# Dispatch tables of two MoE layers from 16-bit one-hot factors, with the tile as the innermost dimension

## The reference

```python
# layer 1
probs = softmax(x @ router_w.T)
w, sel = top_k(probs, 2);  w = w / sum(w)
out = sum over e of combine[:, e, None] * ((silu(x @ g[e]) * (x @ u[e])) @ d[e])
# layer 3: sigmoid router, relu experts with biases, plus a shared feed-forward
scores, idx = top_k(sigmoid(flat @ router_w.T), 2);  w = scores / (sum(scores) + 1e-6)
routed = sum over e of comb[:, e, None] * (relu(flat @ ew1[e] + eb1[e]) @ ew2[e] + eb2[e])
# both: x = x + tanh(g_ffn[l]) * out
```

## Time and profile before

| | us |
|---|---|
| three runs | 1659.20, 1656.66, 1650.44 (median 1656.66) |
| profiled execution, its own time | 1657.25 |
| its span, first to last instruction | 1655.5 |
| busy in the span: PE, PEld | 1409.8 (85%), 1303.3 (79%) |
| DVE, ACT, POOL | 1240.4 (75%), 765.6 (46%), 336.8 (20%) |
| mean granted TensorE clock | 0.906 of full |

### The profile page before, as it was taken

One profiled execution on the slowest core, in us unless ns is written; L12 is line 12 of the kernel. 1 busy time (PEld: TensorE's weight loads), 2 busy tenths in 40 slices (PEclk: granted clock), 3 DMA queues, 4 the chain that ended last, 5 costly groups with the idle time before them and its releaser, 6 DMA issues.

```text
span 1655.5 us, 26047 instructions
## 1 busy us (share of the span) xinstructions
PE 1409.8 (85%) x9986; PEld 1303.3 (79%) x9986; DVE 1240.4 (75%) x2386; ACT 765.6 (46%) x1306; POOL 336.8 (20%) x278
## 2 busy tenths in 40 slices
PE   4897998798996499999489558977999999999995
PEld 4786887586896389999379458966888888999995
DVE  5696778677795679998379779976885857888883
ACT  4445441013454167666355442316454225767673
POOL 2241001000000147765200000000000002445342
PEclk9897997799997589998799879988997999999997
DMA  4232100000002178887400000000002006777883
GB/s 138 89 103 91 41 1 1 1 0 10 1 1 108 52 249 233 241 227 214 127 1 1 7 1 1 1 3 8 1 1 103 1 32 256 218 227 209 227 240 114
DMA packets 44927, 148.24 MB, mean 90 GB/s; under 512 B 11651, under 2 KB 22582, under 8 KB 35062
## 3 DMA queue, kind: packets, MB, share of 16 engines
q1 hardware_dynamic: 28886, 122.04, 21.5%
q0 software_dynamic: 15936, 24.78, 7.7%
HBM read 126.03 MB, written 22.87 MB: 90 GB/s over the span
## 4 chain that ended last, share of the span: by engine, by line
PE 57%; DVE 25%; ACT 7%; issue 5%; DMA 3%; POOLq 1%; SPq 1%; POOL 0%; ACTq 0%; DVEq 0%
PE PS L307 36%; PE PS L1006 6%; PE PS L967 3%; PE PS L990 3%; DVE RA L1597 2%; PE PS L1072 2%; PE PS L1223 1%; DVE RA L1666 1%; DVE FA L1634 1%; ACT RA L1590 1%; PE PS L283 1%; PE PS L999 1%; DVE RA L1646 1%; PE PS L983 1%; ACT Y L225 1%
## 5 line engine op out<-in xcount | busy, mean ns | idle before, releaser
L307 PE MATMUL PS<-RA 128*128 128x256 f32 (+3 forms) x6204 | 945.7, 312 | 78.7 <-DVE RA L398 17.4
L307 PEld LDWEIGHTS PS<-RA 128*128 128x128 f32 x6204 | 862.0, 198 | 133.9 <-issue 34.2
L1524 POOL DMA_INDIRECT sum_rows<-Y,KT x78 | 158.2, 2028 | 191.1 <-ACT Y L1565 163.0
L271 POOL TENSOR_TENSOR rstd<-vareps,neghalf 128x4 f32<-128x4 f32 x36 | 36.8, 1023 | 712.2 <-DVE vareps L208 333.9
L1006 PE MATMUL PS<-VBF,FA 128*128 128x136 f32 x1024 | 137.4, 288 | 4.2 <-ACT FA L772 3.9
L1513 POOL DMA_INDIRECT Y<-normed_rows,KT x78 | 90.0, 1154 | 235.6 <-DVE KT L1316 170.7
L1006 PEld LDWEIGHTS PS<-VBF,FA 128*128 128x128 f32 x1024 | 126.1, 194 | 10.2 <-ACT FA L772 6.6
L772 ACT ACTIVATE FA<-PS 128x1024 f32<-128x1024 f32 x64 | 65.7, 1027 | 105.3 <-PE PS L967 105.3
L1597 DVE TENSOR_TENSOR RA<-FA,RA 128x2048 fp32r<-128x2048 f32 x46 | 105.3, 2288 | 8.5 <-ACT RA L1557 7.9
L1543 ACT ACTIVATE FA<-PS,unit_bias 128x256 f32<-128x256 f32 (+1 forms) x184 | 71.7, 445 | 78.4 <-PE PS L307 65.4
L1666 DVE TENSOR_TENSOR RA<-FA,RA 128x1024 fp32r<-128x1024 f32 (+1 forms) x46 | 80.9, 1759 | 24.8 <-ACT RA L1590 24.8
(11 more groups left out here) (292 smaller groups left out, 1917.4 us busy)
## 6 DMA issues: line engine op xcount, KB each, us to landing
FA<-in_eup SPq DMA_DIRECT2D x46, 1024.0 KB, 7.4
FA<-in_edown SPq DMA_DIRECT2D x23, 1024.0 KB, 6.6
FA<-in_edown SPq DMA_DIRECT2D x23, 512.0 KB, 4.1
FA<-in_fside SPq DMA_DIRECT2D x16, 512.0 KB, 3.5
sum_rows<-X SPq DMA_DIRECT2D x2, 2048.0 KB, 8.2
normed_rows<-Y SPq DMA_DIRECT2D x2, 2048.0 KB, 7.5
fp_rows<-FA POOLq DMA_DIRECT2D x6, 352.0 KB, 6.7
FA<-fp_rows SPq DMA_DIRECT2D x1, 2112.0 KB, 12.2
```

The costliest lines, as they stand in the source:

```text
L307: ins = pe.matmul(dst, stat(a, k), mov(b, k), start=(first and n == 0), stop=(last and n == len(todo) - 1))
L1524: pool.indirect_dma_start(out=sum_rows, in_=rows_out[p][:, t, :], in_offset=None, compute_op=ALU.add, out_offset=bass.IndirectOffsetOnAxis ...
```

## The change

The one-hot factors become 16-bit (bf16), and the tile becomes their innermost dimension: `lane_hot` is (k, lane, tile) and `col_hot` (part, column, tile). The two values of a column become five (`PARTS_OF_ROW`), each exact in 16 bits: the token as its partition number and its tile number plus 1, the weight as a high, a middle and a low part (`split_weights`, four operations that are new on VectorE's path, in layer 1 after `places_of_rows`, in layer 3 after `accumulate(0, 3)`). A set of factors is now three operations: a mask over 39 x 16 columns and tiles, one product of the mask with all five parts (5 x 39 x 16 = 3120 elements), and one lane comparison (128 x 16 = 2048). It signals `hot` once. TensorE runs one instruction per product, with 195 moving columns in place of 78; the elements of one tile are 16 elements (32 bytes) apart in both operands. `write_tables` puts the parts together again in nine operations. GpSimd's constants are written out over the tiles (2048, 624 and four of 16 elements).

```diff
+PARTS_OF_ROW = 5
...
@@ -1163,18 +1166,26 @@
...
-                self.lane = c[:, 0:P]
-                self.column = c[:, 128:128 + NROWS]
-                self.token = c[:, 176:176 + NT]
+                self.parts = c[:, 0:80].bitcast(BF16).rearrange("p (k v t) -> p k v t", k=2, v=PARTS_OF_ROW)
...
-                self.lane_hot = self.xn_all.rearrange("p t d -> p (t d)").rearrange("p (k t n) -> p k t n", k=2, n=P)
                 self.apart = router.kind == "top"
-                self.col_hot = [fview(3072 if self.apart else 7168, NT, 2, NROWS), fview(7168, NT, 2, NROWS)]
+                yf = self.xn_all.rearrange("p t d -> p (t d)")
+                self.lane_hot = yf[:, 0:NT * P].bitcast(BF16).rearrange("p (k n t) -> p k n t", k=2, n=P)
+                hots = PARTS_OF_ROW * NROWS * NT // 2
+                hot_of = lambda v: v.bitcast(BF16).rearrange("p (v c t) -> p v c t", v=PARTS_OF_ROW, c=NROWS)
+                first_hot = hot_of(yf[:, NT * P:NT * P + hots])
+                self.col_hot = [first_hot, hot_of(fview(7232, hots)) if self.apart else first_hot]
+                self.lane = fview(4096 if self.apart else 7168, NT * P // 2).bitcast(BF16).rearrange("p (n t) -> p n t", n=P)
...
+                self.mask = yf[:, NT * P + hots:NT * P + hots + NROWS * NT // 2].bitcast(BF16).rearrange("p (c t) -> p c t", c=NROWS)
...
@@ -1194,9 +1205,11 @@
...
-                pool.iota(self.lane, [[1, P]], base=0, channel_multiplier=0, allow_small_or_imprecise_dtypes=True)
-                pool.iota(self.column, [[1, NROWS]], base=0, channel_multiplier=0, allow_small_or_imprecise_dtypes=True)
-                pool.iota(self.token, [[1, NT]], base=1, channel_multiplier=NT, allow_small_or_imprecise_dtypes=True)
+                pool.iota(self.lane, [[1, P], [0, NT]], base=0, channel_multiplier=0, allow_small_or_imprecise_dtypes=True)
+                pool.iota(self.column, [[1, NROWS], [0, NT]], base=0, channel_multiplier=0, allow_small_or_imprecise_dtypes=True)
+                for k in range(2):
+                    pool.iota(self.parts[:, k, 0, :], [[0, NT]], base=0, channel_multiplier=1, allow_small_or_imprecise_dtypes=True)
+                    pool.iota(self.parts[:, k, 1, :], [[1, NT]], base=1, channel_multiplier=0, allow_small_or_imprecise_dtypes=True)
...
@@ -1217,10 +1230,10 @@
                 pe.matmul(self.counts(1), self.ones, both, start=True, stop=True).then_inc(self.counted, 1)
...
             def sum_tables(self, pe, k):
+                pe.wait_ge(self.hot, 2 * self.turn + k + 1)
                 for t in range(NT):
-                    if t % (NT // 2) == 0:
-                        pe.wait_ge(self.hot, 4 * self.turn + 2 * k + t // (NT // 2) + 1)
-                    ins = pe.matmul(PS[:, 7, 0:2 * NROWS], self.lane_hot[:, k, t, :], self.col_hot[k][:, t].rearrange("p v c -> p (v c)"),
+                    ins = pe.matmul(PS[:, 7, 0:PARTS_OF_ROW * NROWS].rearrange("p (v c) -> p v c", v=PARTS_OF_ROW),
+                                    self.lane_hot[:, k, :, t], self.col_hot[k][:, :, :, t],
                                     start=(k == 0 and t == 0), stop=(k == 1 and t == NT - 1))
                 ins.then_inc(self.summed, 1)
...
@@ -1287,33 +1300,42 @@
                     steps(dve.tensor_reduce(self.posf[:, k, :], self.pick, AX, ALU.add))
                 steps(dve.tensor_copy(rows_of[:, :, :], self.posf))
                 steps(dve.tensor_scalar(self.col_u.bitcast(U32), rows_of[:, :, :], 7, None, ALU.logical_shift_right))
-                steps(dve.tensor_copy(self.col_f, self.col_u.bitcast(U32)))
-                steps(dve.scalar_tensor_tensor(self.lane_f, self.col_f, -float(P), self.posf, ALU.mult, ALU.add))
+                steps(dve.tensor_copy(self.col_b, self.col_u.bitcast(U32)))
+                steps(dve.scalar_tensor_tensor(self.lane_b, self.col_b, -float(P), self.posf, ALU.mult, ALU.add))
...
             def one_hot(self, dve, steps, k):
                 dve.wait_ge(self.normed_out, 16 * (self.turn + 1))
                 if k and not self.apart:
                     dve.wait_ge(self.summed, 2 * self.turn + k)
-                wide = [P, NT, NROWS]
-                hot = self.col_hot[k]
-                steps(dve.tensor_tensor(hot[:, :, 0, :], self.column.unsqueeze(1).to_broadcast(wide),
-                                        self.col_f[:, k, :].unsqueeze(2).to_broadcast(wide), ALU.is_equal))
-                steps(dve.tensor_tensor(hot[:, :, 1, :], hot[:, :, 0, :], row_weight[:, k, :].unsqueeze(2).to_broadcast(wide), ALU.mult))
-                dve.tensor_tensor(hot[:, :, 0, :], hot[:, :, 0, :], self.token.unsqueeze(2).to_broadcast(wide), ALU.mult)
-                half = [P, NT // 2, P]
-                for q in range(2):
-                    ts = slice(q * NT // 2, (q + 1) * NT // 2)
-                    dve.tensor_tensor(self.lane_hot[:, k, ts, :], self.lane.unsqueeze(1).to_broadcast(half),
-                                      self.lane_f[:, k, ts].unsqueeze(2).to_broadcast(half), ALU.is_equal).then_inc(self.hot, 1)
+                if k:
+                    dve.wait_ge(self.hot, 2 * self.turn + k)
+                wide = [P, NROWS, NT]
+                of_columns = lambda v: v.unsqueeze(1).to_broadcast(wide)
+                steps(dve.tensor_tensor(self.mask, self.column, of_columns(self.col_b[:, k, :]), ALU.is_equal))
+                every = [P, PARTS_OF_ROW, NROWS, NT]
+                dve.tensor_tensor(self.col_hot[k], self.mask.unsqueeze(1).to_broadcast(every),
+                                  self.parts[:, k].unsqueeze(2).to_broadcast(every), ALU.mult)
+                dve.tensor_tensor(self.lane_hot[:, k], self.lane, self.lane_b[:, k, :].unsqueeze(1).to_broadcast([P, P, NT]),
+                                  ALU.is_equal).then_inc(self.hot, 1)
+
+            def split_weights(self, dve, steps):
+                steps(dve.tensor_copy(self.parts[:, :, 2, :], row_weight[:, :, :]))
+                steps(dve.tensor_tensor(self.left, row_weight[:, :, :], self.parts[:, :, 2, :], ALU.subtract))
+                steps(dve.tensor_copy(self.parts[:, :, 3, :], self.left))
+                steps(dve.tensor_tensor(self.parts[:, :, 4, :], self.left, self.parts[:, :, 3, :], ALU.subtract))
...
             def write_tables(self, dve, steps):
                 dve.wait_ge(self.summed, 2 * self.turn + 2)
-                ids, weights = PS[:, 7, 0:NROWS], PS[:, 7, NROWS:2 * NROWS]
-                dve.tensor_scalar(source_of, ids, -1.0, 0.0, ALU.add, ALU.max)
-                steps(dve.tensor_scalar(self.empty, ids, 0.0, None, ALU.is_equal))
+                lanes, tiles, high, middle, low = (PS[:, 7, v * NROWS:(v + 1) * NROWS] for v in range(PARTS_OF_ROW))
+                dve.tensor_copy(weight_of, low)
+                steps(dve.tensor_copy(self.ids, tiles))
+                dve.tensor_scalar(self.empty, self.ids, 0.0, None, ALU.is_equal)
+                dve.tensor_tensor(weight_of, weight_of, middle, ALU.add)
+                steps(dve.scalar_tensor_tensor(self.ids, lanes, float(NT), self.ids, ALU.mult, ALU.add))
+                dve.tensor_scalar(source_of, self.ids, -1.0, 0.0, ALU.add, ALU.max)
                 steps(dve.tensor_tensor(self.empty, self.empty, self.unused, ALU.mult))
-                dve.tensor_copy(weight_of, weights)
-                dve.scalar_tensor_tensor(target_of, ids, -1.0, self.empty, ALU.add, ALU.add).then_inc(self.tables, 1)
+                dve.tensor_tensor(weight_of, weight_of, high, ALU.add)
+                dve.scalar_tensor_tensor(target_of, self.ids, -1.0, self.empty, ALU.add, ALU.add).then_inc(self.tables, 1)
                 dve.wait_ge(self.tables, self.turn + 1)
...
         def route(l, kind):
@@ -1356,6 +1378,7 @@
                 router.weigh(dve, steps)
                 dispatch.blocks_of_experts(dve, steps)
                 dispatch.places_of_rows(dve, steps)
+                dispatch.split_weights(dve, steps)
                 for k in range(2):
                     dispatch.one_hot(dve, steps, k)
                 handover["first_up"](dve)
```

More of the change, by code:

```diff
@@ L1165, in __init__ @@
                 c = spare_const
-                self.lane = c[:, 0:P]
-                self.column = c[:, 128:128 + NROWS]
-                self.token = c[:, 176:176 + NT]
+                self.parts = c[:, 0:80].bitcast(BF16).rearrange("p (k v t) -> p k v t", k=2, v=PARTS_OF_ROW)
+                self.lane_b = c[:, 80:96].bitcast(BF16).rearrange("p (k t) -> p k t", k=2)
+                self.col_b = c[:, 96:112].bitcast(BF16).rearrange("p (k t) -> p k t", k=2)
+                self.left = c[:, 112:144].rearrange("p (k t) -> p k t", k=2)
+                self.ids = c[:, 144:144 + NROWS]
                 self.unused_pairs = c[:, 192:192 + NROWS + 1].rearrange("p (b h) -> p b h", h=BR // P)
@@ L1171, in __init__ @@
                 self.col_u = c[:, 240:272].rearrange("p (k t) -> p k t", k=2)
-                self.col_f = c[:, 272:304].rearrange("p (k t) -> p k t", k=2)
```

(8 more changed lines are left out.)

## The result

The changed kernel took 1662.66 us (median of 20 runs, 1657.21 to 1664.9) against 1655.27 for the kernel before (20 runs, 1649.82 to 1660.12): ratio 1.0043, 95% interval 1.0032 to 1.0055, or 7.1 us slower. The forecast was 1649.9 us. The profiled execution's span grew from 1655.5 to 1663.1 us.

The account below looks back on a forecast made before the run. Bound: first layer by VectorE's start plus TensorE's 32 products, second by TensorE's time per product. First layer -4.8 and second -2.0, together -6.8 on 1657.25, gave 1650.4; the runs' median, 0.6 lower, made it 1649.9 us (range 1643.5 to 1660).

Parts of the forecast that it names:

- TensorE: one instruction per product: Table sums, both MoE layers: one 195-column instruction replaces two, 159 ns a product at 2.4 GHz, 246 at 1.2.
- surcharge for the moving columns' step: TensorE's table products: 0.31 ns for each of 195 columns, 61 ns a product, taken from VectorE's stepped rows.
- The scaling by clock: TensorE's table products: unbroken columns scaled by 1.89 from 2.4 to 1.2 GHz, 98 to 185 ns a product.
- Rival B: Table products, both layers: TensorE pays VectorE's whole step rate, 326 ns at both clocks; sum +1.2 us, 1657.9; chance 0.17.
- VectorE's pace: Factor sets: 16-bit operations at 0.52 ns an element; mask 0.48, product 1.78, lanes 1.22 us, a set 3.44.
- The first layer's logic: First MoE layer: VectorE's first set, then TensorE's 32 products in 7.87 us, then tables; 4.8 us gained.
- The weight split: VectorE, four small operations: 0.88 us on the first layer's path, hidden in 1.36 us of idling in the second.
- The tables: Table writing: nine operations take 1.58 us, +0.70 on the first layer's path, inside 10.7 us of room in the second.
- Rival C: VectorE's factors: 16-bit operations run no faster, a set takes 6.45 us; sum +0.3 us, 1657.0; chance 0.06.
- Rival D: TensorE's products: the stepped weight load isn't hidden, 540 ns a product; sum +14.9 us, 1671.6; chance 0.06.
- Rival A: TensorE's products: the step costs nothing, 98 and 185 ns a product; sum -10.1 us, 1646.6; chance 0.26.
- Rival E: Behind the first layer's tables: its gain is swallowed downstream, say by weight loads; -2.0 us, 1654.7; chance 0.09.

Follow-up runs that it names:

- the doubled pairs: Changed kernel with tile outermost, each token's number stored twice, 40 unbroken columns a part: 1643.82 us, ratio 0.9944 to the kernel before.
- the plain kernel: Changed kernel with tile outermost, one copy of each token's number repeated by a step of zero, 195 unbroken columns: ratio 0.9974 to the kernel before.
- the two-tile kernel: Changed kernel with two tiles innermost instead of sixteen, so TensorE steps over 4 bytes, no number doubled: ratio 0.9951 to the kernel before.
- the 565.39 window: First-layer profile window of the changed kernel with six groups of 16 extra products ahead of the second half in both layers; whole time not compared.

## Why the prediction was wrong

**The step that failed is "TensorE: one instruction per product"**, in its surcharge for the moving columns' step: 0.31 ns a column was taken, for 159 ns a product at 2.4 GHz and 246 at 1.2. Measured: 359 and 364. A column costs 1.8 to 1.9 ns, which lies outside even the upper bound, VectorE's whole 1.67 (326 ns). The surcharge came from VectorE's rows; TensorE pays about four times its unbroken 85 ns. Its base was misread as well: the 14 elements of L1233 that stood for contiguous ones are seven pairs whose two values lie 32 bytes apart (line 1250 of the kernel before turns the two dimensions round), and they took 176 ns, so VectorE's own price of such a step was not settled by these rows. The scaling by clock was wrong too: a product with the 32-byte step takes about as long at either clock (359 ns mostly at 1.00, 364 at 0.50), while an unbroken one depends on it (16 in 1.39 us at 1.00 with the doubled pairs; in 2.81 at 0.50 in the plain kernel's first layer). The prediction's own sum turned to a loss from 308 ns a product; with the measured products it gives 11.66 + 5.75 + 5.76 - 19.7 = +3.5 us.

**Its consequence, the clock, was priced nowhere.** Of the 7.1 us in the second layer, 4.45 are the products (5.75 + 5.76 - 2 x 3.53) and the other 2.7 are the unchanged matmuls behind them at the lower granted clock. They bring the prediction's sum from +3.5 to +6.2, where the two stretches have +6.1. Rival B had the first part (+3.4), and with it the right mechanism, one pace at either clock; it came to only +1.2 in sum because its 326 ns were too low (+3.4 for +4.45, and -2.2 in the first layer where -1.1 arrived), and because it lacked the second part.

**What held.** VectorE's pace: 0.49, 1.78 and 1.15 to 1.22 us against 0.48, 1.78 and 1.22. The first layer's logic (VectorE's first set, then TensorE's 32 products, then the tables) is the chain after, with 364 put for 246 ns. The weight split: 0.87 us on the path in the first layer; in the second it goes into the idle time of the earlier trace rows, which shrinks from 1.36 to 0.67 us:

```profile
1316.38 0.17 DVE L1322 CAST VD<-row_weight 128x32 bf16<-128x32 f32 x1
...
1317.89 0.43 DVE L2314 CAST RA<-FA 128x512 fp32r<-128x512 f32 x1 [0.67 <-ACT FA L2284]
```

The tables took 1.40 us (568.14 to 569.54) for 1.58, and in the second layer they stayed in their room: the gather starts at 1368.92, and its rows are first used at 1379.18. Rival C falls with the 1.78 us. Rival D's cause falls with the free load step, though its side, slower, was right. Rival A is the two-tile kernel in all but layout: with the step gone its 98 ns are 85 to 91, and its -10.1 us lie within what that kernel measured (-8.1, -11.4 to -4.6). Rival E, the first layer's gain swallowed downstream, does not hold where that gain is large: with the doubled pairs the second layer alone would give -4.3 us, and -9.3 (-12.7 to -6.0) were measured. For the change's own 1.1 us it stays open.

The Trainium skill (SBUF — State Buffer, Specifications (TRN2)) was cited for its 16-byte lines that want two hits each. Its sign was right and was weighed too lightly: it stood against the layout, and the chip was worse than any row. Its condition of two hits does not hold for TensorE here: steps of 8 bytes make two hits in a line and already cost double (174 against 87 ns). That 16 and 32 bytes, each a new line at every element, cost alike (346 and 352) agrees with it.

## What to carry to other kernels

A layout that suits the engine that writes an operand has to be priced on the engine that reads it, with that engine's own row; where no trace has such a row, the bound must not be borrowed from another engine. Here both are served by a short innermost run: two 16-bit elements keep VectorE's pace (1783 ns for 3120 elements, as with sixteen) and put TensorE's columns 4 bytes apart, which costs it next to nothing (87 to 91 ns a product against 85). Where a change slows a stream of matmuls as the 32-byte step did here, look at the granted clock behind it, and add what the work behind it costs at the lower level.

## What the chip showed that was not expected

- TensorE's moving operand, 195 16-bit columns: 85 ns unbroken, 87 by 4 bytes, 174 by 8, 346 by 16, 352 by 32; the stationary operand by 32 bytes: no more than unbroken.
- The granted clock fell from 1.00 to 0.50 during 5.75 us of products with the 32-byte step, with TensorE counted busy all the time; it held through 5.5 us of unbroken ones.
- In the first layer 13.95 us of busy 32-bit products ran at 0.50 from end to end; behind a group of 16 unbroken 16-bit products (2.53 us) the clock stood at 1.00 for the next group (the 565.39 window above).
- A GpSimd gather that started 0.85 us into a 2.29 us VectorE operation took 2.51 us instead of 1.20.
